# One-core transformer block, attention stage: the row sum's factor, the placing of q's and k's turns, and who makes the outputs' low halves

## What is computed

```python
q = einsum('bse,ehd->bshd', x, wq); k = ...wk; v = ...wv      # x is (1, 1024, 256)
qn = q * rsqrt(mean(q*q) + 1e-6) * q_scale                     # the same for k with k_scale
scores = einsum('bqhd,bkhd->bhqk', qn, kn)
attn = softmax(scores, axis=-1)
out = einsum('bhqk,bkhd->bqhd', attn, v)
return einsum('bqhd,hde->bqe', out, wo)
```

## Time and profile before

| | |
|---|---|
| Median of 3 runs | 1116.76 us (1113.09 to 1117.54) |
| The profiled execution | 1118.01 us, span 1116.2 us |
| PE busy | 959.0 us, 86% of the span |
| DVE busy | 847.2 us, 76% |
| ACT busy | 634.7 us, 57% |
| POOL busy | 475.3 us, 43% |
| Attention's exponentials (L1181) | first at 165.6 us, last at 714.9 us |

### The profile page before, as it was taken

How to read it: one execution, slowest core, us unless ns; L and a number is a source line. 1 busy time by engine, 2 the same in 40 slices (tenths; PEclk the granted TensorE clock), 3 DMA queues, 4 the chain that set the end, 5 groups by cost and what they waited for, 6 DMA issues and landing times. The chain is left out here.

```text
span 1116.2 us, 18350 instructions
## 1 busy us (share of the span) xinstructions
PE 959.0 (86%) x6414; PEld 594.4 (53%) x6414; DVE 847.2 (76%) x1446; ACT 634.7 (57%) x1097; POOL 475.3 (43%) x385
## 2 busy tenths in 40 slices
PE   5976976999989899899989999699789689799697
PEld 4465753555555555555555554278334265577344
DVE  3868339999999999999999989535699746464267
ACT  3655146777777777778777877513511037456341
POOL 3121547445564456644565423030284016532273
PEclk9975989999999999999999999899989879999898
DMA  5575016877888777877878777911023067678632
GB/s 179 107 195 165 1 43 109 162 137 145 166 164 157 133 156 159 165 147 143 149 164 161 148 134 151 225 33 56 21 85 123 5 196 218 196 222 271 200 97 85
DMA packets 380881, 155.61 MB, mean 139 GB/s; under 512 B 287556, under 2 KB 378230, under 8 KB 380534
## 3 DMA queue, kind: packets, MB, share of 16 engines
q1 hardware_dynamic: 363286, 131.23, 53.6%
q10 hardware_dynamic: 14432, 14.81, 4.0%
q0 software_dynamic: 3072, 8.39, 2.2%
HBM read 60.93 MB, written 23.72 MB: 76 GB/s over the span
## 5 line engine op out<-in xcount | busy, mean ns | idle before, releaser
L941 DVE SCALAR_TENSOR_TENSOR a_halves<-a_ex,a_share,a_halves 128x1024 f16<-128x1024 f32 x128 | 194.0, 1515 | 34.9 <-ACT a_halves L935 32.0
L935 ACT ACTIVATE a_halves<-a_ex,a_share 128x1024 f16<-128x1024 f32 x128 | 147.1, 1149 | 68.3 <-DVE a_share L1244 62.8
L1027 POOL TENSOR_TENSOR a_rnorm<-a_ss,a_power 128x8 f32<-128x8 f32 x32 | 67.9, 2120 | 240.6 <-DVE a_ss L1214 240.5
L1238 DVE TENSOR_REDUCE a_nmax<-psum 128x1 f32<-128x1024 f32 x128 | 156.5, 1223 | 6.4 <-PE psum L1107 6.3
L1181 ACT ACTIVATE a_ex<-psum,a_nmax 128x1024 f32<-128x1024 f32 x128 | 142.8, 1115 | 0.2 <-DVE a_nmax L1238 0.2
L1089 PE MATMUL psum<-a_wh,xT_h 128*128 128x128 f16 (+1 forms) x512 | 115.3, 248 | 18.7 <-DVE a_qkTl L1226 15.6
L1090 PE MATMUL psum<-a_wl,xT_h 128*128 128x128 f16 (+1 forms) x512 | 115.1, 247 | 0.0
L1091 PE MATMUL psum<-a_wh,xT_l 128*128 128x128 f16 (+1 forms) x512 | 115.0, 247 | 0.0
L1119 PE MATMUL psum<-a_pT,a_vh 128*128 128x512 f16 x256 | 102.1, 399 | 10.8 <-DMA a_pT<-a_halves 10.8
L1120 PE MATMUL psum<-a_pT,a_vh 128*128 128x512 f16 x256 | 101.9, 398 | 0.0
L1121 PE MATMUL psum<-a_pT,a_vl 128*128 128x512 f16 x256 | 101.1, 395 | 0.0
(11 more groups left out here) (390 smaller groups left out, 2431.1 us busy)
## 6 DMA issues: line engine op xcount, KB each, us to landing
block_outputs<-g_e_ym ACTq DMA_DIRECT2D x16, 512.0 KB, 3.6
split_rest<-a_e_wh SPq DMA_DIRECT2D x15, 384.0 KB, 3.4
wf<-in_L_ffn_W_gate SPq DMA_DIRECT2D x32, 128.0 KB, 2.6
wf<-in_L_ffn_W_up SPq DMA_DIRECT2D x32, 128.0 KB, 2.5
wf<-in_L_ffn_W_down SPq DMA_DIRECT2D x32, 128.0 KB, 3.0
g_rows<-sorted_tokens SPq DMA_DIRECT2D x16, 256.0 KB, 4.2
g_e_raw<-in_L_ffn_wg SPq DMA_DIRECT2D x32, 128.0 KB, 3.1
g_e_raw<-in_L_ffn_wu SPq DMA_DIRECT2D x32, 128.0 KB, 3.4
```

The costliest lines, as they stand in the source:

```text
L935: act.activation(halves[i % PB][:, :, 0, :], ex[m % 2][:, :].rearrange("p (k q) -> p k q", q=P), ACT.Copy, scale=share[:, m:m + 1]).then_i ...
L941: dve.scalar_tensor_tensor(halves[i % PB][:, :, 1, :], ex[m % 2][:, :].rearrange("p (k q) -> p k q", q=P), share[:, m:m + 1], halves[i % P ...
L1238: dve.tensor_reduce(nmax[:, k:k + 1], score_banks(m), AX.X, ALU.max, negate=True).then_inc(max_ready, 1)
```

## The change

Four edits in `attention0`. (1) The row sum's factor becomes `tensor_scalar` with two operations, times 1/4096 and plus 0, so the one-column tensor `unit_share` is gone. (2) `MADE`: turn 6 moves from step 3 to step 1, turn 7 from 3 to 2, turn 8 from 4 to 3, turn 9 stays at 4; v unit 4 moves from 1 to 2 (behind turn 7), v unit 5 from 2 to 4 (behind turn 9). (3) The output's low half is made by PE and ACT: after ACT has taken the high half, PE adds to the same bank the product of -4096 times the identity (`minus`) and the high half, at the end of steps 3 and 7, and ACT copies what is left, at steps 4 and 0 (one head on). Only the very last outputs keep DVE's way. (4) POOL splits the later chunk ahead of the head's weights.

```diff
-    MADE = {0: (1, (3,)), 1: (1, (4,)), 2: (1, (5,)), 3: (1, (6, 7)), 4: (1, (8, 9)),
+    MADE = {0: (1, (3,)), 1: (1, (6,)), 2: (1, (7, 4)), 3: (1, (8,)), 4: (1, (9, 5)),
             5: (2, (0,)), 6: (2, (1,)), 7: (2, (2,))}
-    OUT_AT = {2: 0, 6: 1}
+    OUT_AT, REST_AT, LOW_AT = {2: 0, 6: 1}, {3: 0, 7: 1}, {4: (1, 0), 0: (2, 1)}
...
+        def rest_of_outputs(pe, t, g):
+            pe.wait_ge(o_high, 2 * t + g + 1)
+            pe.wait_ge(minus_ready, 1)
+            pe.matmul(psum[:, O_BANKS[g], :], minus[:, :], oT_h[:, t, g * HALF:(g + 1) * HALF], start=False, stop=True,
+                      skip_group_check=True).then_inc(o_rest, 1)
+        def rest_outputs(act, t, g):
+            act.wait_ge(o_rest, 2 * t + g + 1)
+            act.activation(oT_l[:, t, g * HALF:(g + 1) * HALF], psum[:, O_BANKS[g], :], ACT.Copy, scale=1.0 / PROB).then_inc(o_low, 1)
...
+                    if t < later.CHUNKS:
+                        later.split(pool, t)
                     if t + 3 < H:
                         split_weights(t + 3, (t + 3) % 2, (t + 3) // 2 + 1, unit_count(t, last_v))
-                    if t < later.CHUNKS:
-                        later.split(pool, t)
...
+                        if m in REST_AT and t > 0:                       # PE, after the step's values
+                            rest_of_outputs(pe, t - 1, REST_AT[m])
...
+                        if m in LOW_AT and t >= LOW_AT[m][0]:            # ACT, before tile_high
+                            rest_outputs(act, t - LOW_AT[m][0], LOW_AT[m][1])
...
-                    dve.tensor_tensor(part[:, m:m + 1], total[:, m:m + 1], unit_share[:, :], ALU.mult).then_inc(part_ready, 1)
+                    dve.tensor_scalar(part[:, m:m + 1], total[:, m:m + 1], 1.0 / PROB, 0.0, ALU.mult, ALU.add).then_inc(part_ready, 1)
...
-                        if m - 1 in OUT_AT and t > 0:
-                            low_outputs(dve, t - 1, OUT_AT[m - 1])
```

More of the change, by code:

```diff
@@ L898, in attention0 @@
         nmax = tmp("nmax", [P, 2])
+        minus = tmp("minus", [P, P], F16)
         total, part, share = (tmp(n, [P, QT]) for n in ("total", "part", "share"))
-        unit_share = tmp("unit_share", [P, 1])
         ex = [tmp(f"ex{b}", [P, T]) for b in range(2)]
@@ L906, in attention0 @@
         wo_loaded = sem("a0_wol")
+        minus_ready, o_rest = sem("a0_mi"), sem("a0_or")
         turned = [sem(f"a0_tu{b}") for b in range(PB)]
         (scale_ready, made, high_done, low_done, ss_ready, var_ready, pow_ready, r_ready, qkn_ready, s_ready, max_ready,
-         exp_ready, unit_ready, part_ready, share_ready, p_high, p_low, pv_ready, o_high, o_low) = (
+         exp_ready, part_ready, share_ready, p_high, p_low, pv_ready, o_high, o_low) = (
             sem("a0_" + s) for s in (
-                "sc", "mu", "hi", "lo", "ss", "vr", "pw", "rr", "qn", "s", "mx", "ex", "us", "pa", "sh", "ph", "pl", "pv", "oh", "ol"))
+                "sc", "mu", "hi", "lo", "ss", "vr", "pw", "rr", "qn", "s", "mx", "ex", "pa", "sh", "ph", "pl", "pv", "oh", "ol"))
         def heads(head):
@@ L1201, in _ @@
                 heads(head)
+                rest_outputs(act, H - 2, 1)
                 high_outputs(act, H - 1, 0)
@@ L1263, in head @@
                             squares(t + 2, 0, unit_count(t, ("side", 2, 1)))
-                        if m - 1 in OUT_AT and t > 0:
-                            low_outputs(dve, t - 1, OUT_AT[m - 1])
-                dve.memset(unit_share[:, :], 1.0 / PROB).then_inc(unit_ready, 1)
-                dve.wait_ge(unit_ready, 1)
+                dve.tensor_scalar(minus[:, :], env["ident16"][:, :], -PROB, None, ALU.mult).then_inc(minus_ready, 1)
                 for half in range(2):
@@ L1278, in _ @@
                 heads(head)
+                dve.wait_ge(o_low, 2 * H - 2)
                 low_outputs(dve, H - 1, 0)
```

## The result

The changed kernel takes 1087.68 us (median of 4 runs, 1084.64 to 1088.90) against 1117.15 us for the kernel before: the ratio is 0.9736, 95% interval 0.9701 to 0.9771, or about 29.5 us less. The profiled execution took 1088.47 us, its span is 1086.6 us. The forecast was 1098.5 us.

The account below looks back on a forecast made before the run. Each head was PE's work plus its waits for DVE: 35.12 - 4.45 + 0.43 + (1.0 to 1.25) + 1.6, 1.3 us less. 14 x 1.3 = 18.2 us, 1118.0 to 1099.8; predicted median 1098.5, range 1075 to 1120 us.

Parts of the forecast that it names:

- What bounds the head: Attention heads: a head of 35.12 us is PE's work, 30.7 us, plus PE's waits for DVE, 4.45 us.
- The factor: Row sum's factor on DVE (L1242): one input of one column no longer stalls beside POOL, saving 2.3 us of DVE a head.
- two bounds: Factor beside POOL: nothing saved (as L1214, eight columns) or 2.3 us a head (as L2100, one column); the latter taken.
- The rival in which it still waits: Factor at steps 3 and 4 still stalls behind POOL: head 35.7 us, total 1125 us, slower; chance 0.11.
- The new waits: PE waits for POOL's normalisations ahead of turn 6 (1.0 to 1.25 us) and turn 8 (1.6 us) in each head.
- The old waits go: PE's waits for DVE ahead of step 4's turns and step 5's qk unit, 4.45 us a head, both vanish.
- The low halves: Outputs' low halves on PE and ACT: DVE loses 1.2 us a head, PE gains 0.43 us on the path.
- the forecast itself: Total gain of 0.9 to 1.8 us a head, 1091 to 1104 us; chance 0.47.
- the first rival: Normalisations in time: POOL's L1027 not caught behind L941, both new waits shrink; 1072 to 1086, say 1080 us; chance 0.23.
- POOL's order: POOL's chunk ahead of the head's weights costs nothing, since those weights are first wanted more than a head later.

Follow-up runs that it names:

- third table: Kernel before plus the new factor and MADE with v unit 4 in step 1, turns 6, 7 in 2, v unit 5 in 3, turns 8, 9 in 4: 1078.25 us.
- the last kernel: Changed kernel with the outputs' low halves on DVE again (steps 3 and 7) and the second squares moved from step 1 to step 0: 1084.62 us, ratio 0.9682.

## Why the prediction was right, and where it was off

- **What bounds the head: right.** It is PE's work plus PE's waits. The head less the waits that PE's rows name is 30.9 to 31.0 us with the low halves on DVE (before 31.0, the factor alone 31.0, new table 30.9, third table 30.9; the last kernel's uneven heads are not counted), and 31.0 to 31.8 us in the kernels with the subtractions on PE. Less DVE work didn't make a faster head: after has 29.6 us of it in 33.63, the kernel with the low halves on DVE again 30.15 in 32.45.
- **The factor: right**, with the right one of two bounds. L2100's one column was the row to go by, L1214's eight columns the one not to. The rival in which it still waits was put at 35.7 us a head with waits of 0.55 and 1.3 us; the runs with the old factor and with two columns gave 36.02 and 36.04, with 0.46 and 1.57.
- **The new waits: right in place and cause**, in size nearly: 1.0 to 1.25 us forecast for turn 6, 0.89 measured; 1.6 for turn 8, 1.54 measured. The power operation caught behind the next L941 took 2.60 us both times, as read off one of them before.
- **The old waits go: right for this kernel**, but the reason given was half of it. The text credited the new table with freeing the banks. With the old table and the other edits in place, one wait is gone and the other halved all the same.
- **The low halves: the part's own sum was right** (0.43 us on PE, DVE down to about 29.5, measured 29.59), and the working had the rest: L964 stood between the squares and L941 and let POOL start first. What the text didn't draw from it is that the edit as a whole costs 1.2 us a head beside the new table.
- **The mis-sized terms.** The head gained 1.48 us, not 1.3 (14 x 0.18 = 2.5 us); head 0 was left out of the sum and gave 3.5 us, since its factors stall too (1.85, 1.42 and 1.42 us before; the factor alone gives 4.4 us there); and 5.2 us lie behind the attention, where no term stood. That is 11.2 of the 11.4 us between 18.2 forecast and 29.6 seen. The median of 1087.68 us lies inside the stated range, but below the 1091 to 1104 of the forecast itself and nearer to the 1080 of the first rival. That rival's mechanism didn't happen: the power operation was caught both times.
- **What was left open.** POOL's order, put at nothing, was never undone alone. TensorE's clock, which falls eight times in the heads before, has no term in the sum; that it cost nothing there is the luck of PE's second wait, as the kernel with the squares of step 7 moved shows.

## What to carry to other kernels

An instruction of one column can cost ten times its length when it reads two tensors while the other engine works on SBUF (1.42 us against 0.15 here); look at the longest instance of a line, not at its median, and rewrite it with one input of one column before moving anything else. When an instruction is removed, ask what it kept apart: here 0.6 us of DVE work that read PSUM let POOL's power operation start first. After the first stall is gone, judge each further edit alone and together with the others: here each of two gave a shorter head (32.45 and 32.95 us) than both together (33.63). And when equal heads have two lengths, look at the granted clock of each before you explain the difference by the code.

## What the runs showed of the hardware

- A `tensor_scalar` from SBUF to SBUF waits for POOL with two columns (1.43 us at two places a head, each to within 0.03 us of a POOL instruction's end) and not with one (139 to 153 ns in 128 of 128, with one operation or with two).
- The hold is one-sided for POOL's short power operation: if it starts first, L942 beside it isn't slowed (430.10, 1.27 us, beside 429.66 to 431.30); if L942 starts first, the power operation takes 2.60 us instead of 1.64.
- L1243, with one tensor in PSUM and one in SBUF, took 740 to 752 ns in all 64 instances of the changed kernel, and POOL was busy beside 49 of them.
- 3.4 us of TensorE at half clock (0.50 granted) cost a head 1.69 us where PE had no later wait (33.18 and 34.87 us), and nothing where it had one (35.11 and 35.11 us).
